# Last pass of a four-layer graph kernel: 124 of 416 edge tiles change from row gathers to one-hot products with table slices

## The reference

```
m_in     = concat(x[src], x[dst], ea)              # 53125 x 384
messages = relu(m_in @ msg_w1 + msg_b1) @ msg_w2 + msg_b2
agg      = segment mean of messages over the receiving node
out      = x + (relu(concat(x, agg) @ upd_w1 + upd_b1) @ upd_w2 + upd_b2)
```

## Time and profile before

| | us |
|---|---|
| median of 3 runs (lowest, highest) | 1445.61 (1442.19, 1445.67) |
| profiled execution, first to last instruction (span) | 1439.0 |
| PE busy | 1244.3 (86%) |
| DVE busy | 873.4 (61%) |
| POOL busy | 802.0 (56%) |
| ACT busy | 558.7 (39%) |
| mean granted TensorE clock, share of full speed | 0.967 |

### The profile page before, as it was taken

The page is one execution under the profiler, slowest core; times in us unless marked ns, Lnnn a source line. Parts: engine busy times, 40 slices in busy tenths (PEclk is TensorE's granted clock), DMA queues, the critical chain, the costliest instruction groups (busy, mean ns, idle before and its releaser), DMA issues. The chain is left out here.

```text
span 1439.0 us, 32565 instructions
## 1 busy us (share of the span) xinstructions
PE 1244.3 (86%) x9639; PEld 909.4 (63%) x9640; DVE 873.4 (61%) x2785; ACT 558.7 (39%) x1466; POOL 802.0 (56%) x844
## 2 busy tenths in 40 slices
PE   6888888888888887898689998999989988888996
PEld 3555555555555555788459997377766666666775
DVE  5778777777777876666686437344444444434433
ACT  7445544444544446960232103233322222222222
POOL 4777777777777773000000000777777777777774
PEclk8999999999999999999989998899999999999997
DMA  9633335333333324787500002745565565555541
GB/s 272 158 101 107 102 109 149 95 108 108 104 106 104 104 73 148 226 245 220 48 1 2 2 1 58 202 135 158 155 157 156 156 158 150 145 144 142 146 113 42
DMA packets 199900, 176.66 MB, mean 123 GB/s; under 512 B 48836, under 2 KB 172470, under 8 KB 199638
## 3 DMA queue, kind: packets, MB, share of 16 engines
q1 hardware_dynamic: 173144, 120.28, 31.2%
q0 software_dynamic: 26624, 54.79, 13.3%
HBM read 134.89 MB, written 38.16 MB: 120 GB/s over the span
## 5 line engine op out<-in xcount | busy, mean ns | idle before, releaser
L2211 POOL DMA_INDIRECT between<-p_table,src_g x416 | 397.4, 955 | 471.2 <-DMA p_table<-n_nm 344.7
L387 PE MATMUL acc<-ones_b 128*128 128x512 bf16 x1599 | 426.1, 387 | 28.7 <-PEq L1426 14.8
L781 POOL DMA_INDIRECT rows_by_block<-h_t,mean_bc x312 | 300.1, 962 | 114.3 <-issue 77.1
L387 PEld LDWEIGHTS acc<-ones_b 128*128 128x128 bf16 x1599 | 142.0, 99 | 129.2 <-issue 39.0
L940 PE MATMUL acc<-n_nm 128*128 128x384 bf16 (+1 forms) x832 | 142.7, 294 | 86.9 <-DVE n_nm L835 86.1
L2321 ACT ACTIVATE between<-acc 128x256 f32<-128x256 f32 x208 | 79.8, 384 | 352.8 <-PE acc L2378 335.1
L870 DVE TENSOR_TENSOR between<-between,acc 128x600 f32 x208 | 161.3, 775 | 64.2 <-issue 53.1
L2410 PE MATMUL acc<-w_msg,between 128*128 128x128 f32 x832 | 184.1, 303 | 0.0
L2248 DVE TENSOR_TENSOR between<-acc,between 128x256 f32<-128x256 f32 x208 | 87.6, 421 | 141.9 <-DMA between<-p_table,src_g 93.9
L2389 PEld LDWEIGHTS acc<-between 128*128 128x128 f32 x832 | 128.7, 197 | 71.0 <-issue 51.6
L940 PEld LDWEIGHTS acc<-n_nm 128*128 128x128 bf16 x832 | 67.0, 97 | 164.9 <-DVE n_nm L835 134.7
(11 more groups left out here) (204 smaller groups left out, 1942.5 us busy)
## 6 DMA issues: line engine op xcount, KB each, us to landing
h_t<-rows_by_block SPq DMA_DIRECT2D x73, 387.0 KB, 3.8
between<-in_edge_attr SPq DMA_DIRECT2D x207, 128.0 KB
h_t<-in_edge_attr SPq DMA_DIRECT2D x78, 256.0 KB, 3.1
between<-in_dst SPq DMA_DIRECT2D x51, 288.0 KB
between<-p_table,src_g POOLq DMA_INDIRECT x416
agg_sum<-in_edge_attr SPq DMA_DIRECT2D x25, 256.0 KB
rows_by_block<-h_t,mean_bc POOLq DMA_INDIRECT x312
rows_by_block<-x_nm SPq DMA_DIRECT2D x1, 4644.0 KB, 19.2
```

Of the source, the lines that this page charges most:

```text
L387: pe.matmul(acc[:, bank * BANK:(bank + 1) * BANK].rearrange("p (a n) -> p a n", n=P), ones_b[:, :], ones_b[:, :].rearrange("p (a n) -> p a ...
L781: pool.indirect_dma_start(rows_by_block, bass.IndirectOffsetOnAxis(ap=place_in_table[:, t:t + 1], axis=0), row_group(g)[:, j, :], None).th ...
L2211: pool.indirect_dma_start(got[:, q, j * D:(j + 1) * D], None, p_table, bass.IndirectOffsetOnAxis(ap=src_g[:, n * G + j:n * G + j + 1], axi ...
```

## The change

The first 124 tiles (15872 edges) leave the pairs of the last pass. In `place_and_count` their rows, now with a second key (`dst` + 1, `KW` = 130), are scattered by 13 ranges of 241 source nodes (`SBN`, `NSB`) into 138 tiles of `rows_by_block`: 12 tiles for each of the first 4 ranges, 10 for the others, with unfilled rows zero. The other 292 tiles go into 335 tiles by blocks of 128 nodes, as before. `sum_blocks` makes 126 reads: 52 for the 138 tiles (of 3 tiles, or 1), with one-hots 241 wide, and 74 for the 335 tiles (of 5 or 4, at the end 3). It also keeps the keys (a copy on POOL), turns them and stores them as bytes in `keys_table`.

The last pass has 146 pairs and 138 tiles. Pairs start 10 steps behind tiles (`OFF`), so 128 steps have both a pair and a tile. For a tile, SP loads its rows, every second time keys as a broadcast, at a range's start the 241 rows of P in two loads of 128 and 113, and 128 rows of Q from a node read into a register; `ROWS2` = 6 buffers hold tiles. DVE makes four one-hots for two tiles and adds 128 columns of sums; PE turns the rows and makes P, Q and W_e parts in one PSUM group. The filling products stay only from step 140 on. POOL gathers for 146 pairs. All loops are written out.

```diff
@@ sum_blocks
-                for j in range(0, n, LR):
-                    reads.append((b, b * CAP + j * P, min(LR, n - j), j == 0, j + LR >= n))
+            for s in range(NSB):
+                for j in range(0, cap2(s), LR2):
+                    reads.append((s, base2(s) + j, min(LR2, cap2(s) - j), j == 0, j + LR2 >= cap2(s)))
...
+                for k in ((3, 3) if n == 6 else (5, 4, 4) if n == 13 else (5, 5, 4)):
+                    reads.append((NSB + b, base1(b) + at, k, at == 0, at + k == n))
...
+                        if u < NSB:
+                            sp.dma_start(rows_in_block[:, q, 0:k, :], rows_by_block[row * P:(row + k) * P, :].rearrange("(j p) w -> p j w", p=P)).then_inc(block_in[q].h, 16)
@@ last pass, SP
+                    def tile_rows(u):
+                        r = u % ROWS2
+                        sp.dma_start(rows2[:, r, :], rows_by_block[u * P:u * P + P, :]).then_inc(tile_in[r].h, 16)
+                        if u % 2 == 0:
+                            tile_keys(u // 2)
+                        if starts(u):
...
+                            sp.dma_start(p_win[:, s % PWINS, 0, :], p_table[c:c + P, :]).then_inc(tile_in[r].h, 16)
+                            sp.dma_start(p_win[0:HIGH, s % PWINS, 1, :], p_table[c + P:c + SBN, :]).then_inc(tile_in[r].h, 16)
+                    def tile_window(u):
+                        first = first_of_tile(sp, u)
+                        sp.dma_start(q_win2[:, u % ROWS2, :, :].rearrange("p k f -> p (k f)"),
...
+                    def load_tile(u):
+                        sp.wait_ge(turn.h, turn.at(u + 3 - ROWS2))
+                        tile_rows(u)
+                        tile_window(u)
...
+                    for m in range(4, HERE):
+                        if m + 2 < TILES_HERE:
+                            load_tile(m + 2)
+                        if m < 4 + RING // 2:
+                            window(2 * (m - 4))
+                            window(2 * (m - 4) + 1)
+                        if m >= RING:
+                            load(m)
@@ last pass, POOL
-                    for n in range(PAIRS):
+                    for m in range(HERE):
@@ last pass, DVE
+                        dve.tensor_scalar(hot_p[:, r, 0, :, :], key[:, :, 0, :], part[:, :], None, ALU.is_equal)
+                        dve.tensor_scalar(hot_p[0:HIGH, r, 1, :, :], key[0:HIGH, :, 0, :], part_high[0:HIGH, :], None, ALU.is_equal)
+                        dve.tensor_scalar(hot_q[:, r, :, :], key[:, :, 1, :], part[:, :], None, ALU.is_equal)
+                        dve.tensor_tensor(hot_s[:, r, :, :], iota[:, :].rearrange("p (a n) -> p a n", a=1).broadcast_to([P, 2, P]),
...
+                    def collect_tile(u, step):
+                        col = first_of_tile(dve, u)
@@ last pass, PE
+                        if t >= TILES_HERE + 2:
+                            stream_ones(pe, T_AT // BANK + t % 2, WARM_SLOT)
...
+                    def product_tile(u):
...
+                        pe.matmul(acc[:, o:o + P], hot_p[:, r, 0, j, :], p_win[:, s % PWINS, 0, :], start=True, stop=False)
+                        pe.matmul(acc[:, o:o + P], hot_p[0:HIGH, r, 1, j, :], p_win[0:HIGH, s % PWINS, 1, :], start=False, stop=False)
+                        for k in range(3):
+                            pe.matmul(acc[:, o:o + P], hot_q[:, r, j, :], q_win2[:, u % ROWS2, k, :], start=False, stop=False)
+                        return pe.matmul(acc[:, o:o + P], turned[:, u % MR, G * P:(G + 1) * P], w_msg[:, 2, :], start=False, stop=True)
```

More of the change, by code:

```diff
@@ L61, with cap2, base2, cap1 @@
 LIMIT = 16.0
[L62 to L66, removed]
+KW = D + 2
+TILES2 = 124
+PAIRS2 = TILES2 // 2
+GROUPS2 = TILES2 // KC
+SBN = 241
+NSB = 13
+NODES2 = 4 * NODES_AT
+BIG = 65536.0
+def cap2(s):
+    return 12 if s < 4 else 10
+def base2(s):
+    return 12 * s - 2 * max(s - 4, 0)
+TILES_HERE = base2(NSB)
+def cap1(b):
+    return 13 if b < 7 else 14 if b < NB - 1 else 6
+def base1(b):
+    return TILES_HERE + 13 * b + max(b - 7, 0)
+SURE2 = (9, 8)
+TAIL1 = 4
 ROWG = 8
 HROWS = 6
-LR = 6
+LR = 5
+LR2 = 3
 LB_IN = 4
+SUM_BANKS = 7
 PRING = 3
@@ L98, in h @@
         branch = Signal.path is not None and not self.everywhere
+        if branch and self.of_other_path is not None:
+            return self.of_other_path.h
         if branch not in self.on_path:
@@ L1120, in _ @@
                 def _(sp):
-                    for r, (b, row, k, is_first, is_last) in enumerate(reads):
+                    for r, (u, row, k, is_first, is_last) in enumerate(reads):
                         q = r % LB_IN
@@ L1232, in _ @@
                 pe.wait_ge(vec.h, vec.at(1))
-                pe.matmul(acc[0:1, 0:5], ones[:, 0:1], odd[:, :], start=True, stop=True).then_inc(sums.h, 1)
+                pe.matmul(acc[0:1, 0:6], ones[:, 0:1], odd[:, :], start=True, stop=True).then_inc(sums.h, 1)
                 pe.wait_ge(upd_made.h, upd_made.at(2))
@@ new lines, in update_bank, with hid_at, has_pair, has_tile @@
+            def update_bank(m):
+                return M_AT + m % MR * BANK + G * D
+            def hid_at(k):
+                return hid_of[:, 0, :] if k % 3 == 0 else hid_more[:, k % 3 - 1, :]
+            def has_pair(i):
+                return 0 <= i < HERE
+            def has_tile(u):
+                return 0 <= u < TILES_HERE
+            def collects(step):
+                return min(max(step - 4, 0), TILES_HERE) + min(max(step - OFF - 8, 0), HERE)
+            superblock = [s for s in range(NSB) for _ in range(cap2(s))]
@@ L2131, in sum_window_messages, with starts, loads_until @@
+            def starts(u):
+                return u == base2(superblock[u])
+            def loads_until(u):
+                return sum(32 + 16 * (v % 2 == 0) + 32 * starts(v) for v in range(u % ROWS2, u + 1, ROWS2))
             with nc.Block(no_gpsimd_drain=True) as block:
@@ L2196, in _ @@
+                    for k in range(sum(i < HERE - RING for i in second_in), len(chunks)):
+                        store(k)
                     sp.wait_ge(added.h, added.at(CHUNKS_HERE + LAST - 1))
```

697 lines of the change are left out of this document (452 added, 245 removed).

## The result

The changed kernel takes 1576.2 us (median of 4 runs, 1572.9 to 1588.7) against 1445.6 us beside it: a ratio of 1.091, 95% interval 1.085 to 1.097. The profiled executions are 1575.8 and 1439.0 us, so 136.8 us more.

What follows compares the result with a forecast made beforehand. POOL's gathers bound the last pass before; after the change SP's load queue would. Last pass +58 and `sum_blocks` +50 make 108 us on a span of 1439.0; 1445.6 + 108 = 1554 us, range 1500 to 1640.

Steps and rivals of the forecast that it cites:

- SP's queue sets the last pass: Last pass: SP's loads issue in series, 3.80 us a combined step, 120 steps 456 us; the span ends 58 us later.
- The start of the pass: Last pass before the combined steps: SP's first tile and pair loads, from 922.7 us to 976.4 us; 61.1 us forecast.
- The last steps: End of last pass: 18 steps with pairs and filling at 2.02 us, 36 us, and two with a product alone, 4.
- PE and DVE late next: Combined steps: PE needs 2.5 us and DVE 3.0, both under SP's 3.8; if SP were free, DVE is late next.
- The 113-row load taken as 0: Slices of P at 13 ranges: landing 3.3 us late if moved by one engine, swallowed by the rings' lead, so 0.
- the rival's 43 us: Last pass: the 113-row load is not hidden, 13 x 3.3 us, +43, 1597 us; chance 0.05.
- `sum_blocks` at +50: `sum_blocks`: smaller reads through the same 4 buffers, bound by rounds, 172 us against 120; taken as 50 us more.
- `place_and_count`, taken at 0: `place_and_count`: same 416 scatters, small extra operations under POOL's work, zero stores split; 0, from -5 to +5 us.
- The clock rival: Last pass: without filling PE's clock falls to 1.2 GHz, 5.0 us a step in half of 128 steps, +77, 1631; chance 0.13.
- The middle stages at 0: Stages between `sum_blocks` and the issue of the last part of `q_table`: no change forecast, 0 us.

Runs made afterwards that it cites:

- e2: Changed kernel with the tile's window of Q and its register load issued from ScalarE's queue, not SP's: 1448.7 us, ratio 1.004.
- e1: Changed kernel with the tile's window of Q read from a fixed address, without SP's register load: 1498.9 us, ratio 1.040.
- e11: e2 plus 128-row slices of P, six `sum_blocks` buffers and both registers first on DVE, without filling in the last 18 steps: 1389.3 us, ratio 0.964.
- e7: On top of e2, DVE loads both registers of a step ahead of the two collects: 1453.3 us, ratio 1.007.
- e10: e2 plus 128-row slices of P and six read buffers in `sum_blocks`: 1398.4 us, ratio 0.971.
- e9: Changed kernel with only the second part of each slice of P read as 128 rows instead of 113: 1567.6 us, ratio 1.085.
- e4: Changed kernel with `sum_blocks` reading through 6 buffers of 4 tiles instead of 4 of 5: 1548.1 us, ratio 1.071.
- e3: Changed kernel with the filling products on PE put back in the steps that have a tile: 1572.4 us, ratio 1.091.
- e5: On top of e2, the second part of each slice of P read as 128 rows instead of 113: 1430.3 us, ratio 0.991.
- e12: Changed kernel with SP loading both registers of a step ahead of its issues: 1825.8 us, ratio 0.983, on a chip where the kernel before took 1857.0 us.

## Why the forecast was right, and where it was short

The forecast was 108 us on the span and 136.8 came; 1576 lies in the range, and the mechanism was the one named.

**SP's queue sets the last pass: right.** Five steps at 3.83 us stand in the trace against 3.80 forecast, with 7.4 us of waits in 473; e2 takes 127 us off by moving one issue, e1 77 by removing one gap. Over all 120 steps, with the output stores among them, the queue took 476 us where the forecast had 459: 3.97 us a step, at the top of the 3.6 to 4.0 that the forecast allowed. This term was short by 17 us, for a reason that it left out: 30 of the issues took more than 0.6 us (up to 2.27), together 18 us above a common one of 0.38. Four of them stand behind slices of P; for the others no cause was found.

**The start of the pass: right.** 60.7 us from the last part of `q_table` to the first combined step, 61.1 forecast.

**The last steps: too low by 2.6 us** (51.9 us from the last pair's window in a combined step to the last add, 49.3 forecast). The forecast took 2.02 us a step from a stretch of the kernel before; here a step with filling takes 2.3 us with PE full, and e11 gives 9.9 us back by dropping the filling. The forecast also took the add at 1422.44 us for the last one; it is the last but one, and the last begins at 1426.67. That did not shift the sum: from the last add but one to the end it is 16.6 us before and 17.4 us in the changed kernel.

**PE and DVE late next.** PE's 2.5 us a step was right. Two tiles' turns in a row in the changed kernel, PE's timeline at full clock and without a stop between them, stand 2.47 us apart:

```profile
1074.37 0.27 PE L2683 MATMUL acc<-ident,n_nm 128*128 128x128 f32 x1
...
1076.84 0.27 PE L2683 MATMUL acc<-ident,n_nm 128*128 128x128 f32 x1
```

DVE's 3.0 was too high. It runs steps of 2.47 us in e2, and e7 and e10 show that its registers cost nothing. The sum for it added a register fetch of 0.64 and half of the one-hots in series on top of waits that overlap. The order was wrong too: with SP relieved, the next stop was the slices of P, then PE.

**The 113-row load taken as 0: close.** Some 3 us of the pass by one trace each, with e9's time unable to say more; the rival's 43 us didn't come. With the cover gone (e2) the same load cost 18 us, so a cover there was.

**`sum_blocks` at +50: right.** DVE's one-hots of the first part run from 561.0 to 631.2 us and those of the second from 632.4 to 734.7, 70 and 102 us, which is what the rounds gave. e4, with two buffers more and other sizes of reads, takes 28 us off. `place_and_count`, taken at 0, gave 1 us: the first one-hots of `sum_blocks` begin at 561.0 us, and at 560.0 before.

**The clock rival: its sign was right, its price wrong.** The clock did fall, to 0.84 to 0.89 in most of the pass, and the forecast gave it 0.13 with +77 us. e3 shows that it costs nothing here. The Trainium skill (TensorE: Matmul & The Clock Gate, "What's actually happening") gives an idle engine the half clock. The prediction read this as no fall for an engine that is never idle for long, and the trace disagrees: PE falls to the half clock 20 times between 1040 and 1510 us, though it is busy in three quarters of that time. Where PE hardly stops (e5 from 1160 to 1350 us, e11 from 1040 to 1280) the clock is 1.00 without filling.

**The middle stages at 0: not settled.** 6.7 us came there in the profiled execution. The same stages took 232.4 to 236.8 us in e1 to e11, against 231.9 in the one trace of the kernel before. So 0.5 to 4.9 us remain, and the rest belongs to this one execution. No run was made for it.

**What the change gave.** The gain was real: POOL lost 124 gathers, 117.5 us of its busy time and 155 us at the pace of the pass before. It had to be paid from a queue with 0.7 us a step to spare, with 2 us. With the tile's window on another queue, slices of 128 rows, more read buffers and no filling, the same change is 3.6% faster than the kernel before (e11); the last two might have helped that one too.

## What to carry to other kernels

Before work is moved off the slowest engine, add up the queue that issues its loads, gaps included: here, at some 0.4 us an issue and 0.75 to 0.95 us more where the address comes from a register, the four or five loads of a step took 4 us and were the bound, though no engine looked full. When that bound is found, move the load with the register to a queue with room and look at the next stop again: what was hidden (here the load of 113 rows and the filling products) can cost its price from then on. And a falling clock cost nothing here while PE did not set the pace; put the work back that holds it up and time it, before repairing it.

## What the runs showed of the hardware

- On SP's queue the issue of the tile's window takes 0.34 us behind its gap (changed kernel) and 0.43 right behind another issue (e1). That is no rule for every load: the tile's rows take 0.33 us right behind another.
- A load whose address comes from a register has 0.75 to 0.95 us ahead of it on SP, of which the register's own load is 0.28 or 0.46 us (medians of the pair's and the tile's). The pair's took 0.46 us once the tile's was gone (e1): taking out 0.9 us of gap gave 0.57 a step.
- The queue stood 3.58 to 3.81 us at the issue behind the first load of 113 rows in seven kernels, and 0.43 or 0.44 behind one of 128 in five; at later ranges this came in some kernels and not in others.
- On DVE a register fetched ahead overlaps other work (0.65 to 0.21 us, e7); on SP two fetches in a row, with the arithmetic on the registers, took 1.43 us together, no less than apart (e12).
- One chip ran the kernel before in 1857 us where the others took 1441 to 1446. A time means something only beside the kernel before on the same chip.
